# The set-up of an attention and expert layer, rewritten: weight buffers, first rows, gates

## Chip, cores and metric

One core of one Trainium2 chip. The metric is the device time of one execution in microseconds (us). Engines: TensorE (PE in the profile, its weight loads PEld), VectorE (DVE), ScalarE (ACT), GpSimd (POOL), and SyncE (SP), whose queue issues all transfers.

## What is computed

```python
mod = (silu(c) @ wmod).reshape(4, 6, 1, 256)
sa, ca, ga, sb, cb, gb = mod[:, 0], ..., mod[:, 5]
ga = (2 * (ga >= 0) - 1) * maximum(abs(ga), 0.25)      # gb alike
h = layernorm(x) * (1 + ca) + sa                       # x: 4 batches x 1024 rows x 256
x = x + ga * (h + attention(layernorm(h) * gamma + beta))    # q, k, v, causal, one head of 256, o_proj
h = layernorm(x) * (1 + cb) + sb
x = x + gb * ffn(h)    # F = 704, silu(gate) * up; 8 experts, top 2, adapters of rank 16 on gate, up, down
```

## The kernel before

Everything is fp32. Each operand of a product is split into a high half (rounded to the type of TensorE's fast path) and a low half (what is left), and each product is three matmuls: high x high, high x low, low x high. The split of a buffer is a ScalarE copy into the high buffer and a subtraction on VectorE or GpSimd into the low one.

A batch is 1024 rows, 8 tiles of 128 (`NT`), in two columns of four tiles (`TC`, `CH` = 512 rows). Each engine has its own program: a set-up, then `body(b, last)` for b = 0 to 3. Order between engines is made by semaphores alone; each engine works its own list in order. The body does the attention row by row (i = 0 to 7: scores, row maximum, exponential, transposes of the probabilities, their split, the product with the values), then the feed-forward part in 36 units of hidden columns; the norms and transposes of the next batch lie between these units.

**The set-up before.** SP's queue brings c, x of batch 0, wmod in two pieces, qkv, o_proj, gamma and beta, then the feed-forward weights, all into stage buffers (`s_wg`, `s_wu`, `s_wd`, ...) that share space with the attention's buffers; `s_ad` lies in `wmask`. TensorE makes the modulation: for each batch c's column, spread over 128 columns (`s_scb`), times wmod gives shift, scale and gates of all rows at once (`modulation(b)`, eight jobs of two or four matmuls); and the two weight products wq.wk and wv.wo. VectorE takes the statistics of the 8 tiles of x (line 841), the reciprocal root by three Newton steps (lines 827 to 829), adds 1 to the scale rows (862), and does the first norm of the first four tiles (lines 927 and 844). The other four are done by ScalarE (573, 578) and GpSimd (487, 488). Then the second statistics, whose Newton steps run on GpSimd (429 to 432), and the normalisation into `xr` (856), which TensorE transposes (1272). VectorE scales the transposed columns with gamma and beta (878), ScalarE copies them to the high half (588), VectorE takes the low half (890). Queries, values and the first scores follow on TensorE.

The weight splits (`SPLITS`, 15 steps): high copies on ScalarE (584), low halves on GpSimd (481) and VectorE (909). All are done, or nearly, when batch 0's attention begins. ScalarE and TensorE wait for the last of them in the body (`weight_lo`). The gates are clamped on VectorE in four steps, `gate(b, step)` (lines 862 to 871): for batch 0 in the set-up, for the next batch in the feed-forward part of the body, at its steps r = 8 and 9. After the set-up GpSimd takes up batch 0's residual, x + ga * h for 8 tiles (448, 449), then the second norm's Newton steps for the first four tiles (`newton(b, LN2_A, ...)`, 429 to 437), whose guess VectorE makes behind row 5 of the attention (815 to 820). ScalarE waits for the result at row 6:

```python
if i == NT - 2:
    act.wait_ge(rstd_ready.sem, rstd_ready.at(b, LN2_A))
    for tile in range(TC):
        normalise(tile, zb[:, tile, :], xr[:, tile, :], z2_ready)
```

Those lines (618) stand ahead of row 7's `probs_high(6)` (660) and `scores_exp(7)` (648). TensorE's list at i = 8: the transposes of these `zb` tiles, then those of row 7's probabilities, then the product of row 6's probabilities.

## Time and profile before

| | us |
|---|---|
| median of 3 runs (lowest, highest) | 689.21 (688.83, 689.48) |
| the profiled execution | 688.73 |
| its span in the trace | 686.9 |
| TensorE busy | 652.9 |
| VectorE, GpSimd, ScalarE busy | 474.2, 377.4, 356.7 |

A row of the profile names the line of the kernel, the engine and the operation, the tile written and the tiles read, and the shape; then the time. "Idle before <- releaser" is how long the engine stood before it, and what ended that. The granted clock is a share of TensorE's full speed of 2.4 GHz.

### The profile page before, as it was taken

To read this page: it belongs to the slowest core of one execution; us is meant where nothing else is said; L and a number is where in the kernel's file an instruction comes from. 1 tells how busy PE (TensorE), PEld (TensorE's weight loads), DVE (VectorE), ACT (ScalarE), POOL (GpSimd) and SP (SyncE) were. 2 spreads that over 40 slices of the span, in tenths; PEclk is the share of its full clock that TensorE was granted. 3 is DMA by queue.
4 is the path that set the end of the run, shared out by engine and by line. 5 is a ranking of instruction groups with operands and counts; after the bars stand their busy time and mean duration, and the time that the engine had idled before them with its cause. 6 is when DMAs were issued, how large, how long until landed. Compare 5 with 4: busy or idle time off the path is not lost.

```text
span 686.9 us, 10710 instructions
## 1 busy us (share of the span) xinstructions
PE 652.9 (95%) x3772; PEld 558.8 (81%) x3772; DVE 474.2 (69%) x1146; ACT 356.7 (52%) x642; POOL 377.4 (55%) x473
## 2 busy tenths in 40 slices
PE   4869999999999999999999999999999999999996
PEld 3559987888879987888878897798888998788885
DVE  5997678478886677658976767747987657637323
ACT  4635455546455546465455446564454546654543
POOL 3785345538577236647576516654765635543644
PEclk9989999999999999999999999999999999999999
DMA  8300020000000020000000001000000000000000
GB/s 311 122 1 1 1 62 0 1 2 31 0 2 31 1 62 0 1 1 32 0 1 32 1 1 62 0 1 18 15 1 1 32 1 1 0 1 1 31 0 32
DMA packets 14054, 15.45 MB, mean 22 GB/s; under 512 B 1328, under 2 KB 12720, under 8 KB 14000
## 3 DMA queue, kind: packets, MB, share of 16 engines
q1 hardware_dynamic: 14000, 14.76, 6.4%
q8 instruction: 30, 0.49, 0.3%
q14 instruction: 24, 0.20, 0.1%
HBM read 10.57 MB, written 4.19 MB: 21 GB/s over the span
## 4 chain that ended last, share of the span: by engine, by line
PE 82%; DVE 12%; issue 2%; POOL 2%; DMA 1%; ACT 1%; DVEq 0%; SPq 0%
PE ps L1263 76%; PE ps L1272 6%; DVE xr L856 2%; DVE hid L1103 1%; DVE rstd L829 1%; DVE zb L844 1%; DMA xs<-in_L_attn_x 1%; DVE xT_lo L890 1%; POOL ring_lo L469 1%; DVE mv L836 1%; DVE tr_full L856 1%; ACT act_s L709 1%; DVE zb L927 0%; DVE stat L841 0%; DVE nr_a L827 0%
## 5 line engine op out<-in xcount | busy, mean ns | idle before, releaser
L469 POOL TENSOR_TENSOR ring_lo<-hid,ring_hi 128x512 fp32r<-128x512 f32 x144 | 189.3, 1319 | 115.9 <-ACT ring_hi L717 115.2
L1103 DVE TENSOR_TENSOR hid<-act_s,ps 128x512 f32<-128x512 f32 x120 | 81.9, 684 | 82.0 <-ACT act_s L709 81.4
L709 ACT ACTIVATE act_s<-ps 128x512 f32<-128x512 f32 x120 | 71.7, 597 | 123.0 <-PE ps L1263 122.4
L717 ACT ACTIVATE ring_hi<-hid 128x512 fp32r<-128x512 f32 (+1 forms) x144 | 90.3, 627 | 16.2 <-DVE hid L1101 8.7
L461 POOL TENSOR_TENSOR xT_lo<-tr_full,xT_hi 128x512 fp32r<-128x512 f32 x28 | 35.9, 1297 | 33.5 <-ACT xT_hi L588 33.5
L1263 PE MATMUL ps<-wdT_hi,ring_hi 128*128 128x256 f32 x192 | 53.6, 285 | 0.0
L1263 PE MATMUL ps<-wdT_lo,ring_hi 128*128 128x256 f32 x192 | 53.2, 282 | 0.0
L1263 PE MATMUL ps<-wdT_hi,ring_lo 128*128 128x256 f32 x160 | 45.2, 282 | 0.0
L1263 PE MATMUL ps<-tm_hi,bgT_hi 128*128 128x512 f32 x96 | 39.5, 411 | 5.7 <-DVE hid L1103 5.7
L1263 PE MATMUL ps<-vv_hi,pT_hi 128*128 128x256 f32 x144 | 43.3, 301 | 0.0
L476 POOL TENSOR_TENSOR xr<-xr,y_gb 128x256 f32<-128x256 f32 x31 | 22.1, 739 | 34.2 <-DVE y_gb L1138 34.2
L1263 PE MATMUL ps<-vv_hi,pT_lo 128*128 128x256 f32 x144 | 40.6, 282 | 0.0
L1263 PE MATMUL ps<-vv_lo,pT_hi 128*128 128x256 f32 x144 | 40.6, 282 | 0.0
L660 ACT ACTIVATE pT_hi<-ps 128x512 fp32r<-128x512 f32 (+3 forms) x48 | 21.7, 488 | 35.1 <-PE ps L1272 34.7
L1006 DVE TENSOR_REDUCE rowmax<-ps 128x1 f32<-128x128 f32 (+7 forms) x32 | 24.1, 754 | 22.6 <-PE ps L1263 22.5
L1263 PE MATMUL ps<-xT_hi,wgT_hi 128*128 128x512 f32 x96 | 38.6, 402 | 0.0
L1263 PE MATMUL ps<-xT_hi,wgT_lo 128*128 128x512 f32 x96 | 38.1, 397 | 0.0
L1263 PE MATMUL ps<-xT_lo,wgT_hi 128*128 128x512 f32 x96 | 37.9, 395 | 0.0
L1263 PE MATMUL ps<-ring_hi,adT_hi 128*128 128x512 f32 x96 | 37.9, 395 | 0.0
L1263 PE MATMUL ps<-tm_lo,bgT_hi 128*128 128x512 f32 x96 | 37.6, 392 | 0.0
L1263 PE MATMUL ps<-ring_hi,adT_lo 128*128 128x512 f32 x96 | 37.6, 392 | 0.0
L1263 PEld LDWEIGHTS ps<-wdT_lo,ring_hi 128*128 128x128 f32 x192 | 36.6, 191 | 1.2
(229 smaller groups left out, 2026.4 us busy)
## 6 DMA issues: line engine op xcount, KB each, us to landing
xs<-in_L_attn_x SPq DMA_DIRECT2D x4, 1024.0 KB, 5.6
out<-xr SPq DMA_DIRECT2D x7, 512.0 KB, 3.0
s_mod<-in_L_wmod SPq DMA_DIRECT2D x1, 1024.0 KB, 8.8
s_qkvT<-in_L_attn_qkv SPq DMA_DIRECT2D x1, 768.0 KB, 10.3
s_wg<-in_L_ffn_Wg SPq DMA_DIRECT2D x1, 704.0 KB, 7.4
s_wu<-in_L_ffn_Wu SPq DMA_DIRECT2D x1, 704.0 KB, 8.6
s_wd<-in_L_ffn_Wd SPq DMA_DIRECT2D x1, 640.0 KB, 7.3
s_mod<-in_L_wmod SPq DMA_DIRECT2D x1, 512.0 KB, 6.9
```

The source lines that it names most:

```text
L461: pool.tensor_sub(dst[1], tr_full[:, q % 2, :], dst[0].bitcast(fp32)).then_inc(tr_lo.sem, 1)
L469: pool.tensor_sub(ring[1][:, place(n), :], hid[:, n % HID, :], ring[0][:, place(n), :].bitcast(fp32)).then_inc(h_lo.sem, 1)
L476: pool.tensor_add(xr[:, i, :], xr[:, i, :], y_gb[:, i % 2, :]).then_inc(out_ready.sem, 1)
L660: nc.scalar.activation(pT[0][:, t % 2, j0:j0 + nj, :].rearrange("p j s -> p (j s)"), ps[:, 4 + e % 2, 0:nj * P], ACT.Copy).then_inc(pt_hi. ...
L709: nc.scalar.activation(act_s[:, n % 2, :], ps[:, 2 * (n % 2), :], ACT.Silu).then_inc(silu_ready.sem, 1)
L717: nc.scalar.activation(ring[0][p0:P, place(n), :], hid[p0:P, n % HID, :], ACT.Copy).then_inc(h_hi.sem, 1)
L829: link(V.scalar_tensor_tensor(y, a, 1.5, y, ALU.add, ALU.mult))
L856: V.tensor_scalar(dst, src[:, i, :], mv[:, i, 0:1], rstd[:, i:i + 1], ALU.subtract, ALU.mult).then_inc(sig.sem, 1)
L1006: V.tensor_reduce(rowmax[:, i:i + 1], banks[:, 0:w], X, ALU.max, negate=True).then_inc(rowmax_ready.sem, 1)
L1103: V.tensor_mul(hid[:, n % HID, :], act_s[:, n % 2, :], ps[:, 2 * (n % 2) + 1, :]).then_inc(h_ready.sem, 1)
L1263: return nc.tensor.matmul(o, w, v, start=start, stop=stop, skip_group_check=True)
L1272: return nc.tensor.transpose(o, src, idn)
```

## The change

The weights are loaded into the buffers that later hold their low halves (`raw` shares space with `low`), so a low half is taken in place; paddings are written before the split rather than after it. There are 12 splits instead of 15, all low halves on GpSimd, after the residual of batch 0, which moves into the set-up. ScalarE makes the high copies 0 to 3 in the set-up, and 4 to 11 in batch 0's attention, at rows 3 to 6 (`BODY_HIGH`). The first norm of all eight tiles is VectorE's, the +1 goes into ScalarE's copy of the scale; the second norm's Newton steps of batch 0's input are VectorE's, its normalisation ScalarE's. The gates of all batches are made as rows of 4 partitions (`mod_row`), transposed, clamped once as 16 columns (`gateT`), spread by ScalarE and multiplied with the unit matrix to fill `bc`; `gate` and its semaphore leave the body. SP's loads are reordered and some are split. The diff, cut to its core:

```diff
+        WEIGHTS = {"wgT": [P, KT, FP], "wuT": [P, KT, FULL], "aT": [P, 2, KT, ER], "bgT": [P, FP], "buT": [P, FP],
+                   "wdT": [P, FT, D], "adT": [P, FT, ER], "bdT": [P, D]}
+        raw_ctx = ExitStack()
+        with raw_ctx:
+            raw = {n: sb(f"{n}_raw", shape, fp32, raw_ctx) for n, shape in WEIGHTS.items()}
+        low = {n: sb(f"{n}_lo", shape, f32r) for n, shape in WEIGHTS.items()}
+        high = {n: sb(f"{n}_hi", shape, f32r) for n, shape in WEIGHTS.items()}
...
+        SPLITS = [(("wg", "wu"), *flat("wgT", k, k + 1)) for k in range(KT)]
+        SPLITS += [(("wu",), *flat("wuT", k, k + 1)) for k in range(KT)]
+        SPLITS += [(("a",), *flat("aT", 0, 2)), (("wr",), s_wr[:, :, :], wrT[0], wrT[1]), (("bd",), *flat("bdT", 0, D)),
+                   (("bg",), *flat("bgT", 0, FP)), (("bu",), *flat("buT", 0, FP)),
+                   (("wd",), *flat("wdT", 0, FT // 2)), (("wd",), *flat("wdT", FT // 2, FT)), (("ad",), *flat("adT", 0, FT))]
+        WEIGHT_STEPS = len(SPLITS)
+        W_D_END, W_AD = WEIGHT_STEPS - 2, WEIGHT_STEPS - 1
+        EARLY_HIGH = 4
+        BODY_HIGH = {3: (4, 5, 6), 4: (7,), 5: (8, 9), 6: (10, 11)}
+        LOADS = {"wu": 2, "bu": 2, "wd": 3, "ad": 3, "a": 2, "ln": 2}
+
+        MOD_BANKS = (0, 1, 2, 3, 7, 2, 3, 7)
...
-            sp.dma_start(xs[:, :, :], x[0].rearrange("(i p) d -> p i d", p=P)).then_inc(x_loaded, 16)
+            load("x", xs[:, 0:TC, :], x[0, 0:CH, :].rearrange("(i p) d -> p i d", p=P))
+            sp.dma_start(xs[:, TC:NT, :], x[0, CH:S, :].rearrange("(i p) d -> p i d", p=P)).then_inc(x_loaded, 16)
...
+                ins = pool.tensor_sub(lo, src, hi.bitcast(fp32))
+                if j in (W_D_END, W_AD):
+
+                    link(ins)
+                    ins = pool.memset((wdT if j == W_D_END else adT)[1][0:FREST, FT - 1, :].bitcast(fp32), 0.0)
+                ins.then_inc(weight_lo, 1)
...
             pool.wait_ge(product_hi, 2)
-            pool.wait_ge(gates_done.sem, gates_done.at(0, 0))
+            pool.wait_ge(mod_copied, 2)
             values_weight(0)
             values_weight_low(0)
             pool.wait_ge(wvo_lo.sem, wvo_lo.at(0, 0))
+            for i in range(NT):
+                pool.wait_ge(first_step, FIRST_ROWS[i])
+                residual(0, i)
+            for j in range(WEIGHT_STEPS):
+                weight_low(j)
+            pool.wait_ge(mod_copied, len(MOD_JOBS))
...
+                if b:
+                    for i in range(NT):
+                        residual(b, i)
+                else:
+                    steps[1] = NT
...
+                if what == "scale":
+                    nc.scalar.activation(bc[:, b, SA, :], ps[:, MOD_BANKS[job], 0:D], ACT.Copy).then_inc(unwaited, 1)
+                    nc.scalar.activation(bc[:, b, CA, :], ps[:, MOD_BANKS[job], D:2 * D], ACT.Identity, bias=1.0).then_inc(mod_copied, 1)
...
                 act.wait_ge(product_ready, j + 1)
                 nc.scalar.activation(w[:, :, :].rearrange("p k d -> p (k d)"), ps[:, 4 + j, :], ACT.Copy,
                                      scale=scale).then_inc(product_hi, 1)
+            mod_row(1)
+            modulation(1)
+            modulation(2)
...
+            act.wait_ge(first_shift, 1)
+            for i in range(TC):
+                first_normalise(i)
+            values_weight_high(0)
+            act.wait_ge(modT_ready, 1)
+            nc.scalar.activation(modT[:, :, :, :].rearrange("p t k b -> p (t k b)"), ps[:, TURN_BANK, 2 * KT * B:4 * KT * B], ACT.Copy).then_inc(modT_copied, 1)
+            modulation(3)
+            modulation(4)
+            modulation(5)
+            act.wait_ge(pads_made, 3)
+            weight_high(0)
+            act.wait_ge(first_shift, 2)
+            for i in range(TC, NT):
+                if i >= TC + 2:
+                    attention_inputs(0, (i - TC - 2,))
+                first_normalise(i)
+            modulation(6)
+            attention_inputs(0, range(KT, KT * NC))
+            modulation(7)
+            queries_values(0, range(4))
+            for j in range(1, EARLY_HIGH):
                 weight_high(j)
...
                         probs_high(0)
                     if i < 2:
                         queries_values(b, (6 + i,))
+                    if b == 0:
+                        for j in BODY_HIGH.get(i, ()):
+                            weight_high(j)
...
             dve.wait_ge(x_loaded, 16)
             first, second = range(TC), range(TC, NT)
-            x_stats(range(NT))
+            x_stats(first)
+            dve.wait_ge(x_loaded, 16)
+            x_stats(second)
             moments(range(NT))
-            V.tensor_scalar(neg_mean[:, TC:NT], mv[:, TC:NT, 0], -1.0, None, ALU.mult).then_inc(first_mean, 1)
             rsqrt(0, NT)
-            dve.sem_inc(first_scale, 1)
             dve.wait_ge(mod_copied, 1)
-            gate(0, 0)
-            settle()
-            dve.sem_inc(first_ca, 1)
             for i in first:
-                mark(V.scalar_tensor_tensor(zb[:, i, :], xs[:, i, :], mv[:, i, 0:1], bc[:, 0, CA, :], ALU.subtract, ALU.mult))
+                ln1_centre(0, i)
             settle()
             for i in first:
-                h_rows(0, i).then_inc(first_h, 1)
+                first_rows(i)
+            dve.wait_ge(gates_turned, 1)
+            g = gateT[:, :]
+            link(V.tensor_copy(g, ps[:, TURN_BANK, 0:2 * KT * B]))
+            mark(V.tensor_scalar(gate_sign[:, :], g, 0.0, 2.0, ALU.is_ge, ALU.mult))
+            link(V.scalar_tensor_tensor(gate_size[:, :], g, -1.0, g, ALU.mult, ALU.max))
+            link(V.tensor_scalar_max(gate_size[:, :], gate_size[:, :], 0.25))
+            V.scalar_tensor_tensor(g, gate_sign[:, :], -1.0, gate_size[:, :], ALU.add, ALU.mult).then_inc(gates_made, 1)
             for i in first:
-                dve.wait_ge(first_h, i + 1)
-                mark(V.bn_stats(stat[:, i, :], zb[:, i, :]))
+                first_stats(i)
             moments(first)
-            guess(0, TC).then_inc(first_guess, 1)
+            mark(guess(0, TC, True))
+            big = [lambda i=i: ln1_centre(0, i) for i in second] + [lambda i=i: first_rows(i) for i in second]
+            settle()
+            for n, small in enumerate(first_newton(0, TC)):
+                mark(small())
+                at = steps[1]
+                if n < len(big):
+                    big[n]()
+                dve.wait_ge(vstep, at)
+            first_shifts(0)
+            for i in second:
+                first_stats(i)
+            moments(second)
+            link(guess(TC, TC, True))
+            for small in first_newton(TC, TC):
+                link(small())
+            first_shifts(TC)
             dve.wait_ge(product_hi, 1)
             V.scalar_tensor_tensor(wqk[1][:, :, :].rearrange("p k d -> p (k d)"), ps[:, 4, :], SCORE_SCALE,
                                    wqk[0][:, :, :].rearrange("p k d -> p (k d)").bitcast(fp32), ALU.mult, ALU.subtract).then_inc(product_lo, 1)
-            for i in second:
-                dve.wait_ge(first_h_pool, i - TC + 1)
-                mark(V.bn_stats(stat[:, i, :], zb[:, i, :]))
-            moments(second)
-            guess(TC, TC).then_inc(first_guess, 1)
-
-            dve.wait_ge(first_rstd, 1)
-            for i in first:
-                normalise(i, zb, z_ready, xr[:, i, :])
-            dve.wait_ge(mod_copied, 2)
-            gate(0, 1)
-            gate(0, 2)
-            weight_low(W_BG)
             dve.wait_ge(loaded["ln"], 32)
             attention_scale(0, range(KT))
...
+            dve.wait_ge(modT_made, 1)
+            queries_values(0, range(6))
...
+            def mod_row(h):
+
+                for t, c0 in enumerate(((2, 5), (3, 4))[h]):
+                    for k in range(KT):
+                        last_mm = mm(ps[0:B, ROW_BANKS[h], t * D:(t + 1) * D], scT[:, k, :], s_mod[:, k, c0 * D:(c0 + 1) * D], k == 0, k == KT - 1)
+                last_mm.then_inc(rows_ready, 1)
...
+            pe.wait_ge(loaded["mod_rest"], 16)
+            mod_row(1)
+            pe.wait_ge(gates_spread, 1)
+            modulation(1)
+            modulation(2)
+            mod_turned(1, modT_ready)
+            for job in range(3, 6):
+                modulation(job)
...
+            pe.wait_ge(mod_copied, 2)
             attention_transposes(0, 0, [xr[:, i, :] for i in range(TC)])
...
```

## Rows read from the trace of the kernel before

**Rows 1.** The page of the kernel before, part 1: busy time of the engines.

```profile
PE 652.9 (95%) x3772; PEld 558.8 (81%) x3772; DVE 474.2 (69%) x1146; ACT 356.7 (52%) x642; POOL 377.4 (55%) x473
```

**Rows 2.** TensorE's largest wait from 50 us on (us, times, longest), and one in the timeline.

```profile
PE ps L1263 <- DVE hid L1103: 5.7, 4, 1.7
...
111.12 0.50 PE L1263 MATMUL ps<-tm_hi,bgT_hi 128*128 128x512 f32 x1 [1.33 <-DVE hid L1103]
```

**Rows 3.** The chain of waits, 0 to 80 us: start, us, what.

```profile
7.32 2.72 DVE stat L841 x8
13.99 3.10 DVE zb L927 x4
17.11 3.44 DVE zb L844 x4
35.74 4.82 DVE xr L856 x4
40.69 1.94 PE ps L1272 x8
```

**Rows 4.** TensorE's timeline: start, us, operation.

```profile
45.80 0.44 PE L1263 MATMUL ps<-xT_hi,wqk_hi 128*128 128x512 f32 x1
52.08 0.22 PE L1263 MATMUL ps<-xT_hi,qT_hi 128*128 128x128 f32 x1
...
79.57 1.03 PE L1272 MATMUL ps<-ident,zb 128*128 128x128 f32 x8
80.44 1.04 PE L1272 MATMUL ps<-ident,probs 128*128 128x128 f32 x8
```

**Rows 5.** VectorE's lines 844 and 829: ns min/median/max, then the mean after 100 us.

```profile
L844 DVE SCALAR_TENSOR_TENSOR zb<-zb,rstd,bc x28: 470/799/1534, 17.1 to 502.4; 128x256 f32<-128x256 f32 x28
...
L829 DVE SCALAR_TENSOR_TENSOR rstd<-nr_a,rstd 128x4 f32<-128x4 f32 x12 | 6.2, 518 | 0.4
```

**Rows 6.** Timeline of VectorE and GpSimd around 108 us, and a gate step at 114.

```profile
106.44 0.29 DVE L1166 TENSOR_SCALAR neg_mean<-mv 128x4 f32<-128x4 f32 x1
108.22 1.29 POOL L469 TENSOR_TENSOR ring_lo<-hid,ring_hi 128x512 fp32r<-128x512 f32 x1 [1.51 <-ACT ring_hi L717]
108.30 1.23 DVE L829 SCALAR_TENSOR_TENSOR rstd<-nr_a,rstd 128x4 f32<-128x4 f32 x1
...
114.03 1.40 DVE L862 TENSOR_SCALAR bc<-bc 128x256 f32<-128x256 f32 x1
```

**Rows 7.** GpSimd: line 481's lengths, residual in 49 to 61.9 us, timeline.

```profile
L481 POOL TENSOR_TENSOR wgT_lo<-s_wg,wgT_hi x2: 1683/1908/2133, 31.4 to 33.1; 128x704 fp32r<-128x704 f32 x2
...
L449 POOL TENSOR_TENSOR xs<-xs,gated 128x256 f32<-128x256 f32 x8 | 5.9, 735 | 0.6
...
71.36 0.20 POOL L429 TENSOR_TENSOR nr_a<-rstd 128x4 f32<-128x4 f32 x1 [9.37 <-DVE rstd L820]
```

**Rows 8.** VectorE's timeline behind row 5 of batch 0's attention.

```profile
70.56 0.17 DVE L815 TENSOR_SCALAR nr_v<-mv 128x4 f32<-128x4 f32 x1
71.52 1.09 DVE L1006 TENSOR_REDUCE rowmax<-ps 128x1 f32<-128x896 f32 x1 [0.23 <-PE ps L1263]
```

**Rows 9.** ScalarE: one high copy's mean, and its timeline at rows 5 to 7.

```profile
L584 ACT ACTIVATE wgT_hi<-s_wg 128x704 fp32r<-128x704 f32 x2 | 1.5, 781 | 0.1
...
68.89 0.21 ACT L648 ACTIVATION_READ_ACCUMULATOR probs<-ps,rowmax 128x1 f32 x1
71.96 0.87 ACT L660 ACTIVATE pT_hi<-ps 128x512 fp32r<-128x512 f32 x2 [2.86 <-PE ps L1272]
73.61 0.21 ACT L648 ACTIVATION_READ_ACCUMULATOR probs<-ps,rowmax 128x1 f32 x1
74.94 2.08 ACT L618 ACTIVATE zb<-xr,shift,rstd 128x256 f32<-128x256 f32 x4 [1.12 <-POOL shift L437]
```

**Rows 10.** Stretches around TensorE's pause: busy us of each engine, granted clock.

```profile
36.50:37.00 0.50, 0.00 (x0) 0.00 (x0) 0.50 (x1) 0.00 (x0) 0.50 (x1) 0.87 0.00 0
43.50:44.00 0.50, 0.50 (x3) 0.36 (x3) 0.50 (x1) 0.48 (x1) 0.50 (x1) 0.80 0.00 0
```

More of the change, by code:

```diff
@@ L327, in adaln_attention_moe_lora, with flat @@
-        W_A, W_R, W_BD, W_BG, W_BU, W_BU_REST, W_D, W_AD = range(EARLY, len(SPLITS))
-        HALVES = len(SPLITS)
-        SPLITS += [("wd", s_wd[:, FT - 1, :], [w[:, FT - 1, :] for w in wdT]),
-                   ("ad", s_ad[:, FT - 1, :], [w[:, FT - 1, :] for w in adT])]
-        W_D_HALF, W_AD_HALF = range(HALVES, len(SPLITS))
-        LATE = len(SPLITS) - EARLY
-        LOADS = {"wd": 3, "ad": 3, "a": 2, "ln": 2}
-        MOD_BANKS = (0, 1, 2, 3, 6, 7, 2, 3)
-        MODT_BANK = 6
+        def flat(name, lo, hi):
+            return [t[name][:, lo:hi] if len(WEIGHTS[name]) == 2 else t[name][:, lo:hi, :] if len(WEIGHTS[name]) == 3 else t[name][:, lo:hi, :, :]
+                    for t in (raw, high, low)]
@@ L339, in adaln_attention_moe_lora @@
+        W_D_END, W_AD = WEIGHT_STEPS - 2, WEIGHT_STEPS - 1
[3 more added lines that the diff above has]
+        MOD_BANKS = (0, 1, 2, 3, 7, 2, 3, 7)
+        MOD_JOBS = (("scale", 0), ("gate", 0), ("scale", 1), ("gate", 1), ("gate", 2), ("gate", 3), ("scale", 2), ("scale", 3))
+        ROW_BANKS = (6, 7)
+        TURN_BANK = 6
+        FIRST_ROWS = list(range(1, NT + 1))
         LAST_PIECES = ((TC, TC + 1), (TC + 2,), (TC + 3,))
@@ L373, in _ @@
+            load("bu", raw["buT"][:, F:FP], Bu[:, FULL:F])
+            for key, dst, src in (("wd", raw["wdT"], Wd), ("ad", raw["adT"], Ad)):
                 load(key, dst[:, 0:FT - 1, :], src[0:(FT - 1) * P, :].rearrange("(j p) n -> p j n", p=P))
@@ L572, in _, with modulation @@
[L572 to L579 removed]
+            def modulation(job):
+                what, b = MOD_JOBS[job]
+                act.wait_ge(mod_ready, job + 1)
+                if what == "scale":
+                    nc.scalar.activation(bc[:, b, SA, :], ps[:, MOD_BANKS[job], 0:D], ACT.Copy).then_inc(unwaited, 1)
+                    nc.scalar.activation(bc[:, b, CA, :], ps[:, MOD_BANKS[job], D:2 * D], ACT.Identity, bias=1.0).then_inc(mod_copied, 1)
+                else:
+                    nc.scalar.activation(bc[:, b, GA:GB + 1, :].rearrange("p t d -> p (t d)"),
+                                         ps[:, MOD_BANKS[job], :], ACT.Copy).then_inc(mod_copied, 1)
@@ L581, in weight_high, with first_normalise @@
             def weight_high(j):
-                key, src, (hi, _) = SPLITS[j]
-                act.wait_ge(loaded[key], 16 * LOADS.get(key, 1))
+                keys, src, hi, _ = SPLITS[j]
+                for key in keys:
+                    act.wait_ge(loaded[key], 16 * LOADS.get(key, 1))
                 nc.scalar.activation(hi, src, ACT.Copy).then_inc(weight_hi, 1)
+            def first_normalise(i):
+                nc.scalar.activation(xr[:, i, :], zb[:, i, :], ACT.Identity, bias=shift[:, i:i + 1], scale=rstd[:, i:i + 1]).then_inc(z_ready.sem, 1)
@@ L955, in _ @@
                 attention_low(q)
-            dve.wait_ge(first_rstd, 2)
-            for i in second:
-                normalise(i, zb, z_ready, xr[:, i, :])
-            gate(0, 3)
-            settle()
-            dve.sem_inc(gates_done.sem, 1)
-            weight_low(W_BU_REST)
             attention_scale(0, range(KT, KT * NC))
@@ new lines, in mod_row, with mod_turned @@
+            def mod_row(h):
+                for t, c0 in enumerate(((2, 5), (3, 4))[h]):
+                    for k in range(KT):
+                        last_mm = mm(ps[0:B, ROW_BANKS[h], t * D:(t + 1) * D], scT[:, k, :], s_mod[:, k, c0 * D:(c0 + 1) * D], k == 0, k == KT - 1)
+                last_mm.then_inc(rows_ready, 1)
+            def mod_turned(h, done):
+                pe.wait_ge(rows_copied, h + 1)
+                for q in range(2 * KT):
+                    last_mm = nc.tensor.transpose(ps[:, TURN_BANK, (2 * KT * h + q) * B:(2 * KT * h + q + 1) * B],
+                                                  mod_rows[:, (2 * KT * h + q) * P:(2 * KT * h + q + 1) * P], ident[0:B, 0:B])
+                last_mm.then_inc(done, 1)
```

278 lines of the change are left out of this document (89 added, 189 removed).

## The prediction, made before the changed kernel was run

> **What bounds the kernel now.** I read the page's busy times first: TensorE is busy for 95% of the span [rows 1], so little can be won while it streams. The list of waits of TensorE from 50 us on say where it doesn't: its largest wait there is for VectorE's hidden products, 5.7 us in four pieces, one a batch; the first ends at 111.12, ahead of that batch's gate steps, which begin at 114.03 [rows 2, 6]. The one stretch in which TensorE is not the bound is the set-up. The chain of waits there is VectorE's own work, from the landing of x at 7.3 us to the last normalised tile at 40.55 us, and TensorE's transposes follow at 40.69 [rows 3]. The first score matmul is at 52.08 us, and from there to the end of batch 0's attention TensorE's line has no gap [rows 4]. I therefore price two things: when the first score matmul comes now, and whether anything that the change moves into batch 0's attention is late for TensorE. All times are those of the profiled execution (688.73 us, span 686.9, so 1.8 around it); it lies 0.48 below the median of the three runs, 689.21.
>
> **A rule that the rows give, and that the rest leans on.** A VectorE instruction that reads two SBUF tensors waits for a GpSimd instruction in flight. The scale-and-add of one tile takes 0.470 us at its shortest and up to 1.534 [rows 5]. The Newton product at 108.30, 0.16 us of work on four numbers, took 1.23 us, and ended with the GpSimd instruction that had begun 0.08 before it and ended at 109.51; a one-input tensor_scalar on four numbers took 0.29 [rows 6] where the like takes 0.17 [rows 8]. An instruction with an input in PSUM doesn't show this.
> The Trainium skill (SBUF — State Buffer, Who interferes with whom) says that both kinds, two SBUF inputs and the two-port mode of tensor_scalar, are locked out for a whole GpSimd instruction. That speaks against moving Newton steps to VectorE beside GpSimd work; by it the sum below stands, and where only the large two-input operations waited, it would be rival 2's. The trace agrees for the two-input steps of rows 5; for the other kind it has only the 0.29.
>
> **Set-up, step by step.** The first half of x has a load of its own, but VectorE waits for the second half's semaphore ahead of both statistics, so the statistics start at about 7.3 as before: 0. Up to the end of the first reciprocal roots nothing changes (13.4). The +1 on the scale rows moves into ScalarE's copy, so centring starts at 13.4 instead of 13.99: -0.6. Four centrings and four scale-and-adds took 3.10 + 3.44 us beside GpSimd's own four tiles [rows 3]; GpSimd is now silent, and at 0.38 from start to start (0.470 less some 0.09 of overlap, an estimate) eight are 3.0: they end at 16.5, -4.0. New: the gate's five small steps, 0.9, to 17.4. Statistics, moments and first guess as before, 2.6, to 20.0. Nine Newton steps interleaved with the eight operations of the second four tiles: 8 x 0.46 + 0.2 = 3.9, plus 1.2 where one meets GpSimd's product for the value weight: first shift at 25.2. Statistics, moments, guess of the second tiles: to 27.7. Then nine linked Newton steps and the shift, 10 x 0.2 = 2.0 us alone. But from 27.6 GpSimd runs the value weight's low half (1.3 us, as 512 columns at 108.22 [rows 6]) and then the eight residuals, now in the set-up, of two instructions of 0.735 or a little more each [rows 7], back to back till about 41. By what rows 5 and 6 show a linked small step gets through once, at best twice, per GpSimd instruction: second shift at 34.2 instead of 29.8. ScalarE then normalises four tiles and makes two high copies between them: last tile at 37.5 (before 40.55). Its two copies of modulation 6 let TensorE go at 38.2; eight transposes, and modulation 7 between them and the queries, end at 41.7. TensorE has idled 8 us then and runs at half its clock (below). The low halves of the second column, VectorE against GpSimd again, come at 44.4, where the third query product waits; it started near 45.8 before [rows 4]. First score matmul at about 50.8: **-1.3 us**. Bounds: nothing sticks and the clock is as before, -6.3 (45.8); GpSimd's first weight split delays more and the clock comes back late, +0.6.
> The moved loads cost nothing: SP issues four more transfers, which puts the weights' landing back by some 2 us, and their first reader is ScalarE at 29 us instead of 16. The merged padding removes GpSimd work ahead of 3.7 us that nothing waits for: 0.
>
> **Batch 0's attention.** Twelve weight splits remain, all low halves now on GpSimd in order, the last eight after ScalarE's high copies at rows 3 to 6 of the attention. Up to row 5 these copies fit: ScalarE stood idle ahead of every row's first copy, 2.86 us ahead of row 6's [rows 9], and gets 1.2, 0.8, 1.6. But behind the last two (indices 10 and 11) hangs a chain. In GpSimd's program the twelve splits stand ahead of the Newton steps of the second layer norm; ScalarE waits for their result behind its copies at row 6, ahead of row 7's exponential; TensorE's transposes of those tiles, and those of row 7's probabilities, wait for ScalarE. In times of the trace before:
> - VectorE's guess starts at 70.56 [rows 8]. GpSimd is then in split 8 (high copy done 69.9, a split of 768 columns is 1.9 us by the 1.683 to 2.133 of 704 columns [rows 7]), to 71.9, and split 9, to 73.8. The guess's steps stick: row 6's maximum starts at 74.2 instead of 71.52, its exponential ends at 76.5 instead of 73.82 [rows 8, 9]. Alone this costs TensorE nothing: it needs it at 76.6.
> - ScalarE's copies 10 and 11, 0.84 each by 0.781 for 704 columns [rows 9]: 77.4, 78.2.
> - GpSimd: split 10 to 79.4, padding 0.4; split 11 to 81.7, padding 0.4: 82.1. Newton steps and shift 3.6 (71.36 to 74.94 [rows 7, 9]): 85.7.
> - ScalarE normalises (2.08), row 6's copies, row 7's exponential with its sum (0.86 + 1.2): from 85.7 to 89.8. TensorE's row-7 transposes stood at 80.44 [rows 4]: **+9.3 us**.
> Bounds: if the guess doesn't stick and splits and paddings are at their shortest, 82.45, so 86.4 against 80.44: +6.0. If also VectorE's column low halves meet GpSimd: +10.
> **Clock.** TensorE's granted clock fell to half (1.2 of 2.4 GHz) 2.6 us into the idle stretch that began at 34.2 and came back 2.9 us after work resumed [rows 10]. The set-up has such a stretch before and after. A new one of some 8 us from 79.6 on means about 2.9 us at half clock: **+1.4** (bounds 0 and 2).
> **Bodies of the later batches.** The gate steps leave VectorE three times, one of them 1.40 us under GpSimd [rows 6]. No wait of TensorE for them shows [rows 2]: 0, at best -1. ScalarE's wait on the splits in each batch had long been met: 0.
> **Sum**: -1.3 + 9.3 + 1.4 = +9.4; 688.73 + 9.4 + 0.48 = **698.6 us** as a median.
>
> **Rivals.**
> 1. VectorE's guess slips through (GpSimd is between splits, or such small steps don't stick in the attention): high copies 2.6 earlier, stall 6.8 to 6.0, clock 1.4, and the set-up gains 1.3 to 6: 690.5 to 696. For it: only one row shows a one-input step waiting. Against: splits 8 and 9 are back to back. Chance 0.21.
> 2. **Faster**: small steps of VectorE don't wait for GpSimd at all. Its place is the Newton steps from 27.7 us: shift 2 at 28.7, tiles at 32. With TensorE's idle stretch shorter, its clock holds and the scores start at 44.0, -8.1; the stall is +6.0 with no fall of the clock: 689.2 - 2.1 = 687.1. It decides from a set-up gain of 6 us and no clock loss. Against: of twelve such Newton steps in the batches the mean is 0.518 us, which is eight at 0.16 and the four that met GpSimd at 1.23 [rows 5]. Chance 0.10.
> 3. The gain and the stall cancel within 1.4 us (set-up -6, stall +6): 689. Chance 0.05.
> 4. More is late than I see (the low halves of the residual stream, a second clock loss): 701 to 703. Chance 0.05.
> The forecast's own case, 696 to 701, has the remaining 0.59.
> A difference under 0.2% (1.4 us) can't be told from none here. Faster by more 0.10, within 0.05, slower by more 0.85. The range 691 to 701 leaves out rivals 2 to 4, 0.20.
>
> **What would show it.** In the changed profile: VectorE's centrings at 0.47 us from 13.4; second-half Newton steps at 0.7 each rather than 0.2 around 28 to 34; first scores near 50.8; ScalarE idle some 7 us ahead of the second-norm normalise, released by GpSimd's shift; TensorE idle as long ahead of the transposes of zb, and PEclk under 1 around 80 to 90; the later batches the same length each. Wrong: no GpSimd-released wait of ScalarE beyond 2 us there, or scores that start before 46.

## The result, and the profile of the changed kernel

The changed kernel takes **697.16 us** as a median of four runs (696.9 to 698.53) against 689.02 (688.75 to 689.48) for the kernel before, measured beside it: a ratio of 1.012, with a 95% interval of 1.0105 to 1.0135. It is slower by 8.1 us. The profiled execution of the changed kernel is the slowest of the four, 698.53 us with a span of 696.7; that of the kernel before has a span of 686.9. So the profiles differ by 9.8 us and the medians by 8.1. Only the profiled execution left a trace, so what made it 1.4 us slower than the median isn't shown.

The page answers to [rows 1] with these busy times:

```profile
PE 657.3 (94%) x3780; PEld 556.7 (80%) x3780; DVE 458.4 (66%) x1146; ACT 360.9 (52%) x646; POOL 368.8 (53%) x442
```

TensorE's waits from 50 us on (us in total, times, longest) answer to [rows 2]. The first one is new, and is most of the result:

```profile
PE ps L1247 <- ACT zb L611: 7.0, 1, 7.0
PE ps L1238 <- DVE hid L1088: 5.3, 4, 1.3
PE ps L1247 <- DVE xr L854: 2.1, 3, 0.7
PE ps L1247 <- DVE tr_full L854: 1.6, 3, 0.5
```

TensorE's timeline in batch 0 answers to [rows 4], and the wait for the hidden products to [rows 2] (start, us, operation, what the idle time before it waited for):

```profile
51.44 0.22 PE L1238 MATMUL ps<-xT_hi,qT_hi 128*128 128x128 f32 x1
...
85.94 1.97 PE L1247 MATMUL ps<-ident,zb 128*128 128x128 f32 x8 [7.04 <-ACT zb L611]
87.89 1.97 PE L1247 MATMUL ps<-ident,probs 128*128 128x128 f32 x8
...
119.61 0.50 PE L1238 MATMUL ps<-tm_hi,bgT_hi 128*128 128x512 f32 x1 [1.32 <-DVE hid L1088]
```

The scores start 0.64 us earlier than before, the transposes of zb 6.37 later, the first wait for hidden products, at 119.61, is 8.49 later, and 9.8 are reached at the end. So there is a small gain in the set-up, a stall of 7 us with something behind it, and a slow drift over the batches.

The chain of waits (start, us, what) shows where the stall comes from; VectorE's rows answer to [rows 8], ScalarE's to [rows 9]:

```profile
69.74 1.22 DVE nr_v L813
70.98 1.77 DVE nr_h L814
73.09 1.00 DVE rowmax L991
74.12 1.10 ACT probs L645 x2
75.22 0.74 ACT wdT_hi L565
76.03 1.84 POOL wdT_lo L469
78.23 1.77 POOL adT_lo L469
84.32 1.58 ACT zb L611 x3
85.94 3.92 PE ps L1247 x16
```

Two one-input steps of the guess took 1.22 and 1.77 us where [rows 8] has 0.17; row 6's maximum, its exponential and the high copies 10 and 11 follow late, then splits 10 and 11 on GpSimd, then (cut short in this list) its Newton steps from 80.23 to 83.78, then ScalarE's normalise, then TensorE. In the set-up, the second half's Newton steps on VectorE stand beside GpSimd's work:

```profile
29.57 1.18 DVE L892 SCALAR_TENSOR_TENSOR nr_a<-nr_a,nr_v 128x4 f32<-128x4 f32 x1
30.79 0.16 DVE L893 SCALAR_TENSOR_TENSOR rstd<-nr_a,rstd 128x4 f32<-128x4 f32 x1
30.98 0.58 DVE L891 TENSOR_TENSOR nr_a<-rstd 128x4 f32<-128x4 f32 x1
...
33.89 0.65 DVE L903 TENSOR_TENSOR shift<-neg_mean,rstd 128x4 f32<-128x4 f32 x1
...
29.46 1.27 POOL L445 TENSOR_TENSOR wvo_lo<-gated,wvo_hi 128x512 fp32r<-128x512 f32 x1 [3.40 <-ACT wvo_hi L608]
30.81 0.74 POOL L436 TENSOR_TENSOR gated<-zb,bc 128x256 f32<-128x256 f32 x1
```

Of the ten steps from 29.37 on one took 1.18, five 0.57 to 0.65 and four 0.16: one step sticks under each GpSimd instruction, until that one ends, and at most one more slips through before the next.

### The profile page after: what moved, and what is told of

Its sections match the earlier page's. It is cut to its first block, busy times and chain, and to the rows that moved or that the text cites. A ratio compares the mean times of both kernels' runs of the same rounds, so it can differ in the third digit from the quotient of the medians.

```text
span 696.7 us, 10693 instructions
## 1 busy us (share of the span) xinstructions
PE 657.3 (94%) x3780; PEld 556.7 (80%) x3780; DVE 458.4 (66%) x1146; ACT 360.9 (52%) x646; POOL 368.8 (53%) x442
## 3 DMA queue, kind: packets, MB, share of 16 engines
q1 hardware_dynamic: 14976, 14.76, 6.5%
## 4 chain that ended last, share of the span: by engine, by line
PE 80%; DVE 11%; POOL 3%; issue 2%; ACT 2%; DMA 1%; SPq 0%; DVEq 0%; ACTq 0%; POOLq 0%
PE ps L1238 74%; PE ps L1247 6%; DVE hid L1088 1%; DMA s_mod<-in_L_wmod 1%; DVE zb L842 1%; DVE rstd L827 1%; DVE xr L854 1%; POOL ring_lo L457 1%; DVE mv L834 1%; ACT act_s L707 1%; DVE nr_h L814 0%; DVE zb L845 0%; DVE nr_a L892 0%; DVE stat L900 0%; POOL nr_a L419 0%
## 5 line engine op out<-in xcount | busy, mean ns | idle before, releaser
L1238 PE MATMUL ps<-tm_hi,buT_hi 128*128 128x512 f32 x96 | 37.9, 395 | 0.0
L1238 PE MATMUL ps<-tm_hi,buT_lo 128*128 128x512 f32 x96 | 37.9, 395 | 0.0
```

The source lines that it names most:

```text
L1238: return nc.tensor.matmul(o, w, v, start=start, stop=stop, skip_group_check=True)
```

## The experiments

Every kernel below was timed in five rounds beside the kernel before. The stretch from the first score matmul to the first wait for hidden products is used throughout as the length of "batch 0's middle": 59.04 us in the kernel before (52.08 to 111.12), 68.17 in the changed one (51.44 to 119.61), +9.13.

### The stall: order, high copies, guess

**e1** moves two splits behind the Newton steps:

```diff
-            for j in range(WEIGHT_STEPS):
+            for j in range(W_D_END):
                 weight_low(j)
...
                     newton(b, LN2_A, 0, TC, it)
+                if b == 0:
+                    weight_low(W_D_END)
+                    weight_low(W_AD)
...
```

> The changed kernel with one edit: the last two splits on GpSimd (10 and 11) and their paddings stand behind batch 0's Newton steps of the second layer norm instead of ahead of them. Theory (the stall is the order of GpSimd's program): the guess ends at 72.9 as now, the shift at 76.5 instead of 83.8, ScalarE normalises right behind its high copies at 76.7, TensorE's transposes of zb wait for nothing at 78.9, the granted clock stays at 1 between 80 and 90, and the splits end at 80.6, ahead of their readers. The 7.0 us wait and about 1.5 of clock go: 688 to 689 us instead of 697.2. Rival 1 (GpSimd has too much work there in whatever order): the wait moves to the weights' or the inputs' low halves, 690 to 693. Rival 2 (the lost time is elsewhere): over 695.

Measured: 688.93 us, ratio to before 1.0006 (0.9997 to 1.0015). The 7 us wait is gone; of TensorE's waits in 50 to 100 us one is left, ahead of row 7's transposes:

```profile
PE ps L1251 <- ACT probs L649: 0.9, 1, 0.9
```

The middle of batch 0 is 60.19 us (50.05 to 110.24): 7.98 of the 9.13 are gone. With the other order of GpSimd's program the stall doesn't come about; rivals 1 and 2 fall.

**e3** leaves the order and brings the high copies forward by a row:

```diff
-        BODY_HIGH = {3: (4, 5, 6), 4: (7,), 5: (8, 9), 6: (10, 11)}
+        BODY_HIGH = {2: (4,), 3: (5, 6, 7), 4: (8, 9), 5: (10, 11)}
```

> The changed kernel with one edit: ScalarE's high copies in batch 0's attention come one row earlier (row 2: 4; row 3: 5, 6, 7; row 4: 8, 9; row 5: 10, 11; row 6: none); GpSimd's order stays, splits ahead of the Newton steps. Theory (GpSimd was waiting for the high copies, 3.3 us ahead of split 10): split 11 and its padding end at 73 instead of 80.3, the guess still sticks until 73, the shift comes at 76.7, nothing is left of the 7.0 us wait and the clock stays up: 688 to 689 us. Rival 1 (two more copies at rows 2 to 5 make ScalarE late for the transposed probabilities, in rows where it stood idle 0.3 to 1.6 us): the stall goes but 1 to 2 us appear as waits of TensorE on pT in rows 3 to 6, 689.5 to 691. Rival 2 (order is all that counts, the splits take as long): 696 to 697.

Measured: 689.71 us, ratio 1.0008 (1.0000 to 1.0017). The stall goes this way too. The time is in rival 1's range, but its waits aren't there: TensorE has none on the transposed probabilities in rows 3 to 6. The 0.9 ahead of row 7's transposes is left as in e1, and 0.4 us is left ahead of zb, since GpSimd's last split keeps the guess and the Newton steps back until 72.5. So it isn't the order alone: the splits stood ahead of the Newton steps *and* their inputs came late, and mending either is enough.

**e2** keeps GpSimd silent during the guess, and changes nothing else:

```diff
             for j in range(WEIGHT_STEPS):
+                if j == W_D_END - 2:
+                    pool.wait_ge(norm_ready.sem, norm_ready.at(0, LN2_A))
                 weight_low(j)
```

> The changed kernel with one wait added: GpSimd waits for the first guess of batch 0's second layer norm before split 8, so that no GpSimd instruction is in flight during VectorE's guess at 69.7; order unchanged. Theory (two of the guess's small steps sit behind 1.84 us splits, 1.22 and 1.77 us instead of 0.17): the steps are at 0.17 to 0.2 again, row 6's maximum comes at 70.9 instead of 73.1, the copies 10 and 11 end at 74.6 instead of 76.7, and the shift at 82.2 instead of 83.8, for all that the splits start 1.8 us later: 695.3 to 696 us instead of 697.2. Rival (the steps take long for another reason than GpSimd's instructions): they stay long, splits only start later, and the time is 698 to 699.

Measured: 696.14 us (694.97 to 696.35), 1.0 below the changed kernel and just above the range that I expected. The steps are short:

```profile
69.38 0.17 DVE L815 TENSOR_SCALAR nr_v<-mv 128x4 f32<-128x4 f32 x1
69.58 0.17 DVE L816 TENSOR_SCALAR nr_h<-nr_v 128x4 f32<-128x4 f32 x1
```

From the first scores to the end of the Newton steps it took 30.46 us (51.08 to 81.54) instead of 32.34 (51.44 to 83.78): 1.9 us for two steps on four numbers, although the splits started later. So it was GpSimd's splits that made them long.

**f1** puts splits 8 to 11 behind the Newton steps, so both are mended:

```diff
-            for j in range(WEIGHT_STEPS):
+            for j in range(W_D_END - 2):
                 weight_low(j)
...
+                if b == 0:
+                    for j in range(W_D_END - 2, WEIGHT_STEPS):
+                        weight_low(j)
...
```

> As e1, but splits 8 to 11 (not only 10 and 11) stand behind batch 0's Newton steps on GpSimd, so that GpSimd is silent during VectorE's guess too. Theory (what is left of the stall in e1, 0.85 us ahead of row 7's transposes, is the guess held up behind splits 8 and 9: row 6's maximum, exponential and the two high copies came 2 us late): guess steps at 0.17, row 6's maximum about 2 us earlier than in e1, no wait of TensorE ahead of row 7's transposes: 0.9 us below e1, 688.0. Rival (four splits, 7.8 us of GpSimd, behind the Newton steps are late for TensorE's wait on the weights or for the inputs' low halves): a new wait there of 1 us or more, 689 or more.

Measured: 688.12 us, ratio 0.9990 (0.9981 to 0.9999). No wait of TensorE is left in 50 to 100 us, and the middle of batch 0 is 59.02 us (51.45 to 110.47), as before the change. The whole +9.13 is accounted for.

### The clock

**g4** keeps TensorE busy in the stall with work whose results are overwritten:

```diff
+        PAD = 28
...
+                        if b == 0:
+                            pe.wait_ge(probs_ready.sem, probs_ready.at(b, NT - 2))
+                            for _ in range(PAD):
+                                mm(ps[:, 0, :], xT[0][:, 0, 0, 0:P], xT[0][:, 0, 0, :], True, True)
                         for k in range(KT):
                             pe.wait_ge(z2_ready.sem, z2_ready.at(b, TC - 1))
```

> The changed kernel with one edit: 28 matmuls of 512 columns, their results overwritten, on TensorE between row 5's probs-times-values and the wait for the normalised tiles of batch 0, some 6.5 us of the 7.0 that it idled there. Nothing is computed earlier for it. Theory (my clock term: the pause drops the granted clock, and the transposes and products behind it run at half speed until 90): the clock stays at 1 from 80 to 90, row 7's transposes take 1.04 us instead of 1.97, and 2.0 us go: 695.2 instead of 697.16. Rival 1 (what follows the stall waits for the other engines and not for TensorE's speed): clock up, time 696.5 to 697. Rival 2 (the clock falls anyway): no change in the clock.

Measured: 695.94 us (695.3 to 696.65), 1.2 below. Stretches of 2 us, whose third number from the end is the granted clock; first the changed kernel:

```profile
82.00:84.00 2.00, 0.00 (x0) 0.00 (x0) 0.00 (x0) 0.19 (x1) 1.31 (x7) 0.79 0.00 0
84.00:86.00 2.00, 0.06 (x1) 0.06 (x1) 0.00 (x0) 2.00 (x5) 0.00 (x0) 0.50 0.00 0
86.00:88.00 2.00, 2.00 (x9) 1.62 (x10) 1.60 (x4) 1.83 (x4) 0.00 (x0) 0.50 0.00 0
88.00:90.00 2.00, 2.00 (x10) 2.00 (x11) 1.61 (x4) 1.22 (x3) 0.59 (x1) 0.51 0.00 0
90.00:92.00 2.00, 2.00 (x19) 2.00 (x18) 1.22 (x2) 1.01 (x2) 1.61 (x2) 1.00 0.01 4
```

and g4's stretch, then its transposes:

```profile
84.00:86.00 2.00, 1.09 (x8) 0.86 (x8) 1.09 (x3) 2.00 (x4) 0.00 (x0) 1.00 0.00 0
...
84.45 1.09 PE L1248 MATMUL ps<-ident,zb 128*128 128x128 f32 x8 [0.72 <-ACT zb L612]
86.39 1.09 PE L1248 MATMUL ps<-ident,probs 128*128 128x128 f32 x8 [0.86 <-ACT probs L646]
```

The clock stays at its upper level (2.4 GHz), and zb's transposes take 1.09 us instead of 1.97; but then TensorE waits 0.86 for row 7's exponential, so that row 7's start 1.94 behind zb's in one kernel and 1.95 in the other. Only what comes after gains: batch 0's middle is 67.23 us (49.92 to 117.15) against 68.17. The clock term is **0.94 us**, not the 2.0 that I expected of this run. The changed kernel ran at half clock for some 4 us after work resumed.

### The set-up

**e4** holds the residuals back until VectorE's Newton steps are through:

```diff
+            pool.wait_ge(first_shift, 2)
             for i in range(NT):
                 pool.wait_ge(first_step, FIRST_ROWS[i])
                 residual(0, i)
```

> The changed kernel with one wait added: GpSimd waits for VectorE's second shift before the eight residuals of the set-up. Theory (VectorE's linked Newton steps on four numbers are held up by GpSimd's 0.73 us instructions): the nine steps and the shift are at 0.16 to 0.2 apiece apart from the one beside the value weight's low half, the second shift is at 31.5 instead of 34.5, TensorE's transposes of the second tiles at 35.6 instead of 38.6, the first score matmul at 48.3 instead of 51.4: 694 us instead of 697.2; the stall behind the splits stays at 7 us. Rival 1 (the residuals, now later, meet VectorE's low halves instead and take the gain back): steps short, first scores at 50.5 or later, 696 to 697. Rival 2 (the steps are slow by themselves): no change in them and 697 or more.

Measured: 695.29 us (694.37 to 695.87), 1.9 below the changed kernel where I had expected 3.2, ratio to before 1.0091. VectorE's steps and the GpSimd instruction that one of them still met:

```profile
28.14 1.16 DVE L894 SCALAR_TENSOR_TENSOR rstd<-nr_a,rstd 128x4 f32<-128x4 f32 x1
29.34 0.16 DVE L892 TENSOR_TENSOR nr_a<-rstd 128x4 f32<-128x4 f32 x1
...
30.51 0.16 DVE L904 TENSOR_TENSOR shift<-neg_mean,rstd 128x4 f32<-128x4 f32 x1
...
28.01 1.27 POOL L445 TENSOR_TENSOR wvo_lo<-gated,wvo_hi 128x512 fp32r<-128x512 f32 x1 [2.91 <-ACT wvo_hi L609]
```

From the first centring to the end of the second shift it takes 17.47 us (13.20 to 30.67) instead of 19.78 (14.76 to 34.54). This is 2.3 us, where I had expected 3.0. The theory holds, both rivals fall, and the stall behind the splits is 7.0 as foretold.

**f2** is f1 and e4 together with the loads reordered:

```diff
+            load("mod", s_mod[:, :, 0:2 * D], wmod[:, 0:2 * D].rearrange("(k p) n -> p k n", p=P))
             load("x", xs[:, 0:TC, :], x[0, 0:CH, :].rearrange("(i p) d -> p i d", p=P))
             sp.dma_start(xs[:, TC:NT, :], x[0, CH:S, :].rearrange("(i p) d -> p i d", p=P)).then_inc(x_loaded, 16)
-            load("mod", s_mod[:, :, 0:2 * D], wmod[:, 0:2 * D].rearrange("(k p) n -> p k n", p=P))
...
-            dve.wait_ge(x_loaded, 16)
+            dve.wait_ge(loaded["x"], 16)
             first, second = range(TC), range(TC, NT)
```

> f1 together with e4 (GpSimd's residuals behind VectorE's second shift) and with the set-up loads in another order: the first piece of wmod is issued ahead of x, and VectorE's first statistics wait for the first half of x by its own semaphore. Theory (the set-up's chain is landing of wmod, TensorE, ScalarE's copy, centring, then the Newton steps): wmod's piece lands 0.7 to 1.5 us earlier than 8.63 to 9.2, centring starts at 12 instead of 13.2 to 13.8, the second shift is at 29.5, TensorE's transposes at 33.5, the first score matmul at 46.5 against 50.05 in e1; with f1's 0.9 that is 4.0 to 4.5 us below e1: 684.5. Rival 1 (x, now behind wmod, lands late and the first roots bound the centring): scores at 47.5, 685.5. Rival 2 (the gains of the set-up are lost again further on): 687.5 or more.

Measured: 686.36 us, ratio 0.9960 (0.9947 to 0.9974). wmod's piece is there at 5.60 us instead of 8.63, yet centring starts at 13.20, as in e4, behind the last of VectorE's nine root steps on x's statistics:

```profile
13.00 0.17 DVE L832 SCALAR_TENSOR_TENSOR rstd<-nr_a,rstd 128x8 f32<-128x8 f32 x1
13.20 1.28 DVE L850 SCALAR_TENSOR_TENSOR zb<-xs,mv,bc 128x256 f32<-128x256 f32 x3
```

So my theory was wrong, and rival 1 was right on what bounds the centring: the two chains, x's and wmod's, end almost together, and mending one bares the other. But the scores didn't start at rival 1's 47.5; they started at 48.77, where e4's started at 47.54. TensorE's transposes began together (34.84 and 34.75), and the granted clock came back later. First f2's stretch, then e4's:

```profile
38.00:40.00 2.00, 2.00 (x4) 0.67 (x2) 1.89 (x3) 0.32 (x1) 1.92 (x3) 0.50 0.00 0
```

```profile
38.00:40.00 2.00, 2.00 (x7) 1.18 (x6) 1.89 (x3) 0.66 (x2) 1.92 (x3) 0.86 0.00 0
```

The time, 686.36, lies between rival 1's and rival 2's for it.

### The batches

**f3** is e1 with the gate steps back in the batches (the values are computed once more, 0 is added where 1 was):

```diff
+                        if r == 8:
+                            dve.wait_ge(out_ready.sem, out_ready.at(b, -1))
+                            gate(b + 1, 0)
+                            gate(b + 1, 1)
+                        if r == 9:
+                            gate(b + 1, 2)
+                            gate(b + 1, 3)
```

> e1 with the removed gate steps of the batches put back on VectorE at their old places (they compute the same values once more, and 0 is added where 1 was), GpSimd's wait for them too. It measures the term that I had put at 0. e1's batches are 160.00 us long, those of the kernel before 159.70. Theory A (these steps lie beside other work): batches of 160.0 again, time as e1, 688.9. Theory B (their removal changed the interplay of the engines so that TensorE is slower): batches of 159.7, 0.9 us below e1, 688.0. Theory C (their removal is a gain that something else eats): batches of 160.2 or more, 689.5 or more.

**f4** is e1 with the order of allocation turned round:

```diff
+        high = {n: sb(f"{n}_hi", shape, f32r) for n, shape in WEIGHTS.items()}
         raw_ctx = ExitStack()
...
         low = {n: sb(f"{n}_lo", shape, f32r) for n, shape in WEIGHTS.items()}
-        high = {n: sb(f"{n}_hi", shape, f32r) for n, shape in WEIGHTS.items()}
```

> e1 with the weights' high halves allocated ahead of their low halves in SBUF (in the changed kernel low first; in the kernel before low and high of each tile side by side); nothing else differs. In e1 TensorE's matmuls of 512 columns on bgT, buT and adT weights follow each other in 0.2318 to 0.2347 us on the mean, in the kernel before in 0.2278 to 0.2299, and e1's batches are 0.3 us longer without any longer wait. Theory (where the weights lie in SBUF sets this pitch): with other addresses the pitch and the batch change, 159.7 us at best, 688.0. Rival (the addresses have no part in it): batches of 160.0 and the pitches of e1, 688.9.

Measured: 689.79 and 689.77 us, ratios 1.0012 (1.0002 to 1.0021) and 1.0013 (1.0004 to 1.0022), e1's 1.0006 within both intervals. Batches, from one wait for hidden products to the next: 160.21, 160.03 and 160.04 in f3, 160.10, 160.00 and 160.12 in f4, 160.00 in e1, and 159.69 and 159.73 for the first two of the kernel before (its third, 160.11, holds a wait of 1.68 instead of 1.33). f3's time is in the range of its theory C, 0.86 above e1, but f4, without the gate steps, is as far above e1, and the batches differ by 0.1. So the removed gate steps were worth nothing that can be told, as I had put them, and their removal isn't what makes the batches longer either. In f4 each weight again began 64 bytes beyond a multiple of 256, so it didn't test what mattered; that was seen only afterwards, in the addresses.

**g1** and **g2** are e1 with pads ahead of tiles (g1 the first and a third of 64 bytes ahead of the ring; g2 all three, the third of 224):

```diff
         s_wr = sb("s_wr", [P, KT, E], fp32)
+        sb("pad_weights", [P, 48], fp32)
...
         SA, CA, GA, GB = range(4)
+        sb("pad_rows", [P, 24], fp32)
```

> e1 with two pads in SBUF: 192 bytes a partition ahead of the weights' low halves and 64 ahead of the ring. What differed in the addresses: in the kernel before bgT, buT, wdT, adT and bdT began at multiples of 256 bytes (wgT, wuT, aT at 128 beyond one) and their matmuls of 512 columns followed each other in 0.2278 to 0.2299 us; in e1 and f4 all weights began 64 beyond a multiple of 256, and the pitch was 0.2318 to 0.2347, as wgT's and wuT's in both kernels. Now all weights, the ring and tm begin at multiples of 256; the stream xT and the rows stay off them. Theory (the alignment of the stationary tile sets the pitch): bgT, buT and adT back at 0.229, wgT and wuT at 0.229 too, batches of 159.5 or less, 687.5 us against e1's 688.93. Rival 1 (it is the moving operand's alignment, xT's for wgT and wuT): bgT, buT, adT at 0.229, wgT and wuT at 0.234, batches of 159.7, 688.0. Rival 2 (alignment has no part in it): 160.0 and 688.9.

> g1 with a third pad of 96 bytes ahead of the modulation rows, so that xs, zb, xr, xT, tr_full and the like begin at multiples of 256 bytes as well. Theory (moving operand): wgT's, wuT's and the scores' matmuls come down to 0.229 too, batches of 159.2 or less, 1.5 us or more below g1. Rival (only the stationary tile, or nothing, counts): as g1 within 0.3 us.

Measured: **687.45** us for g1, ratio 0.9975 (0.9966 to 0.9985), and **684.71** for g2, 0.9941 (0.9927 to 0.9954). The first wait for hidden products in batches 1 and 2, of e1:

```profile
270.24 0.50 PE L1242 MATMUL ps<-tm_hi,bgT_hi 128*128 128x512 f32 x1 [1.31 <-DVE hid L1092]
430.24 0.50 PE L1242 MATMUL ps<-tm_hi,bgT_hi 128*128 128x512 f32 x1 [1.32 <-DVE hid L1092]
```

and of g2:

```profile
270.65 0.50 PE L1245 MATMUL ps<-tm_hi,bgT_hi 128*128 128x512 f32 x1 [1.40 <-DVE hid L1095]
429.61 0.50 PE L1245 MATMUL ps<-tm_hi,bgT_hi 128*128 128x512 f32 x1 [1.41 <-DVE hid L1095]
```

The pitch (mean from one 512-column matmul's start to the next's, over all of the trace from 92 us on) with the tiles' first bytes beyond a multiple of 256. In each pair the stationary tiles, which are loaded as weights, come first, and the moving ones, which stream past them, second. The first bytes are counted from the kernels' allocations, as no trace shows an address:

| kernel | bgT, buT, adT / tm, ring | pitch, ns | wgT, wuT / xT | pitch, ns | batch, us |
|---|---|---|---|---|---|
| before | 0 / 0 | 228 to 230 | 128 / 224 | 231 to 236 | 159.7 |
| e1 | 64 / 0 | 232 to 235 | 64 / 224 | 234 to 235 | 160.0 |
| g1 | 0 / 0 | 228 to 231 | 0 / 160 | 233 to 235 | 159.6 |
| g2 | 0 / 0 | 227 to 231 | 0 / 0 | 227 to 231 | 159.0 |

Six steps in a row show it in the timelines, all without a wait. In e1:

```profile
279.62 0.39 PE L1242 MATMUL ps<-xT_hi,wgT_hi 128*128 128x512 f32 x1
...
281.02 0.40 PE L1242 MATMUL ps<-xT_hi,wuT_hi 128*128 128x512 f32 x1
```

and in g2:

```profile
279.88 0.39 PE L1245 MATMUL ps<-xT_hi,wgT_hi 128*128 128x512 f32 x1
...
281.24 0.39 PE L1245 MATMUL ps<-xT_hi,wuT_hi 128*128 128x512 f32 x1
```

1.40 us against 1.36. That the alignment of tiles sets the batches' length is shown: g1 alone takes 0.4 us off each of e1's, g2 another 0.6. The theory on the stationary tile alone falls with g1, whose wgT stayed slow; that g1's time came out at the theory's 687.5 was luck. g1's rival 1, the moving operand alone, falls with e1, whose bgT was slow on an aligned tm. So it takes both tiles.

What it takes of them these four kernels leave open. Where the pitch was short, both tiles stood at 0; where it was long, they stood at two different offsets. The rule may be that both begin at a multiple of 256 bytes, or that both have the same offset from one. The 28 added matmuls of g4, whose tiles lie as in the changed kernel, speak for the second: their stationary and their moving tile both begin 224 beyond.

```profile
77.21 6.52 PE L1239 MATMUL ps<-xT_hi 128*128 128x512 f32 x28
...
80.00:82.00 2.00, 2.00 (x11) 1.65 (x10) 0.00 (x0) 0.00 (x0) 1.45 (x8) 1.00 0.01 4
```

They follow each other in 0.227 us (27 steps in 6.13), the short pitch, on a tile with which wgT's matmuls took 0.231 to 0.236. They differ from the others also in reading one and the same tile each time, so this isn't proof; no run gave two different tiles one offset other than 0.

### The version put together

**g3** is f1 with e4's wait and g2's pads, without the reordered loads.

> The version put together from what worked: batch 0's Newton steps ahead of splits 8 to 11 (f1), residuals behind the second shift (e4), everything aligned (g2); the loads in the changed kernel's order, since f2 showed that an earlier wmod only bares the roots of x's statistics. From f1's 688.12: 2.3 us for e4's earlier transposes, and whatever g2 gains against e1: 685.8 if alignment gives nothing, 684.8 with 1 us, 683.5 with 2.5 us. Rival (the set-up's gain is lost to a clock that comes back later, as from 34.8 to 40.4 in f2): 687.

Measured: **681.31 us** (680.42 to 682.01), ratio to the kernel before **0.989** (0.9875 to 0.9906): 7.8 us below it and 15.9 below the changed kernel. The first scores stand at 47.34, and the batches are 158.9 us. It beats my 683.5, the sum for an alignment worth 2.5 us; g2 against e1 is worth 4.2, with which the same sum is 681.6. Its busy line:

```profile
PE 649.4 (96%) x3780; PEld 556.7 (82%) x3780; DVE 452.5 (67%) x1146; ACT 360.1 (53%) x646; POOL 368.1 (54%) x442
```

## Why the prediction was right, and which terms were not

The forecast was 698.6 against 697.16, with the sign and the mechanism of the stall as described. By its terms, in the profiled executions, in us:

| term | predicted | measured | shown by |
|---|---|---|---|
| first score matmul | -1.3 | -0.64 | profile; -1.34 over ten profiles |
| stall in batch 0 | +9.3 | +8.19 | e1, f1, e2 |
| clock behind it | +1.4 | +0.94 | g4 |
| batches and end | 0 | +1.3 | profile; e1, g1 |
| sum | +9.4 | +9.8 | |

The table goes by the slowest of the changed kernel's four executions, the only one with a trace. By the medians the stall and its clock are 9.0 (the changed kernel against f1), and f1 is 0.8 below the kernel before, so the set-up's gain and the longer batches come to -0.8 together, where the table has +0.7.

- **Set-up: centring at 13.4.** Mis-sized: it began at 14.76 here, behind wmod's piece, TensorE's products and ScalarE's copies, since TensorE could begin on the piece at 10.19 instead of the 8.83 of before. I had taken only the roots as its bound. In the other profiles with this set-up it began on it at 8.50 to 10.35, and centring began at 13.09 to 14.93, so it is scatter more than a cost of the change. Eight centrings and scale-and-adds at 0.42 each took 3.38 us instead of 3.0, and the stretch to the second shift's end was 19.78 where I had 20.8. Within this term the **sticking of the small steps** was right: e4 shows it, and the second shift's end at 34.54 stands against my 34.2.
- **Low halves and first scores.** The mean of ten profiles with this set-up (after, e1, e2, e3, f1, f3, f4, g1, g2, g4) is 50.74 us against 52.08: -1.34, as predicted. The single one in the table was late. The kernel before has one profile only.
- **The guess under splits 8 and 9.** Right. The row's maximum began 73.09 where my 74.2 less the set-up's 0.64 makes 73.56. The Trainium skill (SBUF — State Buffer, Who interferes with whom) has tensor_scalar contend with GpSimd in its two-port mode: in the kernel before the only row for that was a 0.29. Here there are 1.22 and 1.77 under splits of 1.84, and 0.17 in e2 with GpSimd silent, so the trace agrees.
- **Copies, splits, Newton.** The chain was right link by link. It was too long by a sum of small things: the two high copies end 1.5 after the exponential instead of 1.7, the two paddings take 0.31 and 0.20 instead of 0.4 each, a split 1.84 instead of 1.9. Predicted for row 7's transposes: 89.8 less 0.64; measured: 87.89.
- **Clock.** The mechanism was right. The size was off, as I let all the half-clock time count: the transposes that ran slowly were followed by a wait for ScalarE anyway.
- **Bodies: 0, at best -1.** This step failed, in size and in sign. I priced the instructions that leave and not the tiles that move. The 64 bytes of s_wr now stand ahead of the weights and push bgT, buT, wdT, adT and bdT 64 bytes away from where they lay against tm and the ring. Each batch became 0.3 to 0.4 us longer without a new wait (159.7 before, 160.0 in e1, 160.1 in the changed kernel), and g1, with these tiles put back, has 159.6. No row that I had picked could show it: it is in the starts of TensorE's matmuls, and the lists of waits don't have it.

Rival 1 (the guess slips through) falls with the two long rows. Rival 2 (small steps don't wait) falls with e2 and e4. Rivals 3 and 4 fall with the time. The sum came close partly by luck, by errors that cancel: 1.6 too much in the stall and its clock, 1.3 too little in the batches, 0.7 too much gain in the set-up.

**What stays open.** Profiles with one set-up start their scores between 49.92 and 51.69 us. A part goes with the landing of wmod's piece. Another is when the clock comes back, for which I have no cause. e1's stretches first:

```profile
38.00:40.00 2.00, 2.00 (x9) 1.75 (x8) 1.15 (x2) 0.35 (x1) 1.92 (x4) 0.50 0.04 8
40.00:42.00 2.00, 2.00 (x6) 0.97 (x5) 1.90 (x3) 1.07 (x3) 1.92 (x3) 0.89 0.00 0
42.00:44.00 2.00, 2.00 (x11) 1.59 (x10) 0.89 (x3) 1.10 (x3) 1.92 (x3) 1.00 0.00 0
```

and e2's:

```profile
40.00:42.00 2.00, 2.00 (x4) 0.67 (x2) 1.90 (x3) 0.52 (x1) 2.00 (x2) 0.50 0.00 0
42.00:44.00 2.00, 2.00 (x7) 1.46 (x6) 0.20 (x1) 0.66 (x2) 1.92 (x3) 0.71 0.00 0
```

e1's transposes began at 37.65 and its clock was back by about 40.4; e2's began at 37.04, and it was back after 43. e2's first scores came 1.0 us later, though its transposes had begun 0.6 earlier. Whether the kernel before would gain from pads for xT as well wasn't tried, nor were two tiles with the same offset other than 0.

## What to carry to other kernels

When work moves to another engine's queue, list what stands behind it *there* and whose result the critical engine will ask for: four splits ahead of thirteen tiny steps of a layer norm cost 9 us here, and the tiny steps first gave it all back; and keep GpSimd silent while VectorE does short linked steps that others wait for. After any change of the allocation compare the pitch of the same matmuls in both traces and the first bytes of their tiles: 0.5 KB of pads a partition was worth over 4 us of 689 here.

## What the runs showed of the hardware that I had not expected

- A 512-column fp32r matmul follows the one before in 0.227 to 0.231 us where both its tiles begin at a multiple of 256 bytes, and in 0.231 to 0.236 where the two begin at different offsets from one. With both at the same offset of 224 bytes (g4's pads) it was 0.227.
- The same set-up code had its clock back 2.8 us after work resumed in one execution (e1) and 6 us in another (e2).
- The first piece of wmod, 512 KB, issued at 2.36 us, was there for TensorE between 8.50 and 10.35 us with the same instructions ahead of it.
